# A four-layer graph network on one core: in the first attention layer, the product of a node's own features with its share moves from VectorE to GpSimd

## The reference

```python
s2 = jnp.concatenate([src, ar])          # edges, then one loop from each node to itself
d2 = jnp.concatenate([dst, ar])
...
a = jnp.exp(logit - m[d2])
denom = jax.ops.segment_sum(a, d2, num_segments=n)
alpha = a / denom[d2]                    # the shares, 4 heads
out = jax.ops.segment_sum(alpha[:, :, None] * xl[s2], d2, num_segments=n)
out = out.mean(axis=1) + b_gat
...                                      # normalize, gamma, beta, elu
x = _layernorm(x + that)
```

## Time and profile before

| what | value |
|---|---|
| time of 3 runs, median | 12803.6 us (12781.44 to 12825.93) |
| the profiled execution, its own time | 12791.1 us |
| its span in the trace | 12789.4 us |
| busy over the span: VectorE (DVE) | 6375.9 us, 50% |
| GpSimd (POOL) | 7493.3 us, 59% |
| TensorE (PE) | 6448.9 us, 50% |
| ScalarE (ACT) | 2885.5 us, 23% |
| mean granted TensorE clock | 0.717 of full speed |

### The profile page before, as it was taken

How to read it: one execution, slowest core, us unless ns; L and a number is a source line. 1 busy time by engine, 2 the same in 40 slices (tenths; PEclk the granted TensorE clock), 3 DMA queues, 4 the chain that set the end, 5 groups by cost and what they waited for, 6 DMA issues and landing times. The chain is left out here.

```text
span 12789.4 us, 75437 instructions
## 1 busy us (share of the span) xinstructions
PE 6448.9 (50%) x17662; PEld 2860.9 (22%) x17662; DVE 6375.9 (50%) x12622; ACT 2885.5 (23%) x5100; POOL 7493.3 (59%) x7050
## 2 busy tenths in 40 slices
PE   3432454455555886545454531345665575650276
PEld 1110222222222443222122210122222232330133
DVE  2110254444443333545454568436999994440486
ACT  1210322222222332222221210111000453220143
POOL 4667265666675443657566767666775003557487
PEclk8665777676767998767676765566666897765688
DMA  3520122111112443222222222222111342222243
GB/s 89 152 72 10 43 71 58 53 52 56 55 55 70 164 164 114 74 68 78 69 80 63 82 73 78 57 65 47 35 34 27 122 151 71 59 54 48 70 130 95
DMA packets 899857, 961.94 MB, mean 75 GB/s; under 512 B 480972, under 2 KB 535422, under 8 KB 886866
## 3 DMA queue, kind: packets, MB, share of 16 engines
q1 hardware_dynamic: 674034, 814.55, 19.4%
q0 software_dynamic: 225376, 142.56, 6.2%
HBM read 491.45 MB, written 542.49 MB: 81 GB/s over the span
## 5 line engine op out<-in xcount | busy, mean ns | idle before, releaser
L649 POOL DMA_INDIRECT gathered<-hop,place_of_source x1564 | 1610.4, 1030 | 1141.5 <-DVE weighted L694 474.0
L649 POOL DMA_INDIRECT gathered<-u,place_of_source x1564 | 1665.1, 1065 | 821.9 <-issue 480.0
L708 DVE SCALAR_TENSOR_TENSOR sums<-sums,same_as_before,weighted 128x64 f32<-128x64 f32 x3510 | 997.8, 284 | 193.0 <-DVE sums L708 29.4
L649 POOL DMA_INDIRECT gathered<-x,row_of_source x782 | 799.9, 1023 | 492.9 <-issue 238.6
L670 PE MATMUL bank<-of_first,ident 128*128 128x512 f32 (+1 forms) x1176 | 796.2, 769 | 561.8 <-issue 324.3
L1493 PE MATMUL bank<-glr,pair_turned 128*128 128x512 f32 x782 | 655.1, 935 | 447.9 <-issue 241.9
L435 PE MATMUL bank<-dense_tmp,mean 128*128 128x512 f32 x980 | 634.1, 775 | 448.6 <-issue 304.6
L435 PE MATMUL bank<-dense_a,center 128*128 128x512 f32 x588 | 441.1, 885 | 737.2 <-DVE dense_a L453 356.4
L1885 POOL DMA_INDIRECT out_dram<-attend_out,node_to_write x392 | 561.6, 1433 | 234.4 <-ACT attend_out L1806 114.9
L397 DVE COPY dense_out<-bank 128x512 f32<-128x512 f32 x392 | 261.0, 687 | 835.2 <-remote 712.9
L649 POOL DMA_INDIRECT gathered<-x_with_place,src_index x391 | 405.6, 1037 | 407.4 <-DVE weighted L694 280.9
(11 more groups left out here) (412 smaller groups left out, 14920.0 us busy)
## 6 DMA issues: line engine op xcount, KB each, us to landing
head_sums<-head_sums SPq DMA_DIRECT2D x98, 1024.0 KB
y<-conv_out SPq DMA_DIRECT2D x294, 256.0 KB
conv_out<-y SPq DMA_DIRECT2D x245, 256.0 KB
hop<-sums SPq DMA_DIRECT2D x196, 256.0 KB
cat<-hop SPq DMA_DIRECT2D x196, 256.0 KB
u<-conv_out SPq DMA_DIRECT2D x196, 256.0 KB
x<-dense_out SPq DMA_DIRECT2D x194, 256.0 KB
x<-dense_out SPq DMA_DIRECT2D x97, 272.0 KB
```

The lines of the kernel that those rows point to most:

```text
L649: return e.indirect_dma_start(out=into, out_offset=None, in_=tab, in_offset=bass.IndirectOffsetOnAxis(ap=index, axis=0), bounds_check=top, ...
L708: e.scalar_tensor_tensor(s[:, k, :], b, go[:, t:t + 1], m[:, k, :], ALU.mult, ALU.add).then_inc(st.summed.handle, 1)
```

## The change

The own product is taken out of VectorE's program into a function, `own_product`. In the first attention layer (`v2`) GpSimd calls it for all 49 groups; in the second layer VectorE still does, at the same place. GpSimd's gather `first_heads` stands behind the 49 products. Waits, operands and the semaphore `owned` are the same as before.

```diff
@@ -1820,6 +1820,15 @@
+            def own_product(e, g):
+
+                l, c = g % LANES, slice(g * K8, (g + 1) * K8)
+                if g >= 5:
+                    e.wait_ge(*turned_in(g - 5))
+                e.wait_ge(*(mine_in[l](16 * (g // LANES + 1)) if v2 else lanes[l].loaded[0](16 * (g // LANES + 1))))
+                e.tensor_tensor(heads_of(O[g % 5][:]), each_head(mine[l], K8), per_head(lg[:, HEADS:, c], K8),
+                                ALU.mult).then_inc(owned.handle, 1)
+
@@ -1874,10 +1883,11 @@
                     for g in range(NG):
+                        if v2:
+                            own_product(e, g)
+                            continue
                         if g == NG - 4:
                             first_heads()
-                        if v2:
-                            continue
@@ -1886,7 +1896,9 @@
-                    if not v2:
+                    if v2:
+                        first_heads()
+                    else:
@@ -1917,11 +1929,8 @@
                         steps.to(due(g, 0.6))
-                        if g >= 5:
-                            e.wait_ge(*turned_in(g - 5))
-                        e.wait_ge(*(mine_in[l](16 * (g // LANES + 1)) if v2 else lanes[l].loaded[0](16 * (g // LANES + 1))))
-                        e.tensor_tensor(heads_of(o[:]), each_head(mine[l], K8), per_head(lg[:, HEADS:, c0:c0 + K8], K8),
-                                        ALU.mult).then_inc(owned.handle, 1)
+                        if not v2:
+                            own_product(e, g)
                         steps.to(due(g, 0.8))
```

## The result

The changed kernel takes 13004.34 us (median of 4 runs, 12973.66 to 13025.25) against 12814.76 us for the kernel before, run beside it (4 runs, 12781.44 to 12828.5). The ratio is 1.015, 95% interval 1.012 to 1.0179, or 154 to 229 us slower. The direction was forecast; the size, 81 us on 12803.6, was not, and 13004 lies above the range's 12975.

The account below looks back on a forecast made before the run. VectorE, 97.0% busy, bounds the stage at 14.05 us per group; 11.35 + 4.4 + 0.1 = 15.85 us, 1.80 more over 49 groups, gives +88 us: 12885 us, range 12770 to 12975.

Parts of the forecast that it names:

- exclude each other: GpSimd's product and VectorE's two-input SBUF instructions never overlap, so their times add: 15.85 us per group, +88 us.
- L489 bore it: GpSimd gets in behind the product of features and shares, ahead of L489, which shows longer or idle time before it.
- VectorE's own work: VectorE's work per group in the first attention layer falls from 13.63 to 11.35 us without the own product.
- Rival 1: GpSimd and VectorE run side by side in the first attention layer: -100 us, 12695 us; chance 0.18.
- rival 2: GpSimd's reads go into gaps of VectorE's in the first attention layer: -4 us, 12795 us; chance 0.08.
- The hold: GpSimd's own product of 128x2048 in each group: 4.4 us, the middle between its two bounds.
- the lower end: GpSimd's product takes 2.94 us if its second input costs nothing.
- the upper: GpSimd's product takes 5.8 us if its second input costs as much as the first.
- k: Remainder per group beside VectorE's work and GpSimd's product: between -0.69 and 0.42 us, taken as 0.1.
- come late at VectorE: In the side-by-side case, chains of small steps late in half of the 14.05 us group: -60 instead of -112 us.

Follow-up runs that it names:

- run 4: The change, with GpSimd's product of a group also waiting until VectorE has added group g-2: 15.21 us a group.
- run 1: The change, with the own product left out on both engines and GpSimd filling the heads buffers with zeros once: 13.66 us a group.
- run 8: The change, with eight more 128x512 matmuls per group on TensorE into an unused bank: 17.54 us a group.
- runs 5 to 7: L484 moved behind the next group's product of features and shares, in the kernel before, the change, and the kernel without own product: 14.25, 16.00, 12.07 us a group.
- run 3: GpSimd takes four of the own product's eight columns (128x1024), VectorE the other four at the old place: 16.59 us a group.

## Why the prediction was wrong

**What held.** VectorE was the bound. GpSimd's product and VectorE's two-input steps exclude each other, now shown in both directions. The product came in behind the product of features and shares in three groups of four, and L489 bore it. VectorE's own work fell nearly as said: 11.65 us a group, forecast 11.35 (of the 0.3, 0.16 are the mean over the whole stage, 13.63 in place of 13.79, and 0.14 the product's 2.14 in place of 2.28). Rival 1 (side by side) and rival 2 (in pieces) did not occur.

**The hold was sized too high, 4.4 us.** In the change VectorE's busy time per group is 14.99 - 11.65 = 3.34 us more than without a product, and GpSimd's instruction alone takes 3.68 (run 4). That is 0.7 us above the lower end, 2.94, and 2.1 below the upper, 5.8. The Trainium skill's 4497 ns (GPSIMD Engine Reference, section 3.1), for an add of as many elements, is 0.8 us more than this product with both inputs broadcast took; the measurement decides. By this term alone the forecast would have been 49 x 1.1 = 52 us too high.

**The step that failed is k**, "at most the 0.42 us in which VectorE is idle anyway", taken as 0.1. It was 2.68 us. I bounded the idle time after the change by the idle time before it. But the product that was taken out was also what VectorE did while TensorE and ScalarE worked between L453 and L484. The trace of before had it, first VectorE and then ScalarE, whose L444 gives L484 its input:

```profile
10313.77 0.69 DVE L453 SCALAR_TENSOR_TENSOR attend_a<-attend_a,attend_xT 128x512 f32<-128x512 f32 x1
10314.38 2.04 DVE L1916 SCALAR_TENSOR_TENSOR head_sums<-head_sums,same_as_before 128x256 f32<-128x256 f32 x4
10316.34 2.29 DVE L1923 TENSOR_TENSOR heads<-own_rows,logits 128x2048 f32<-128x2048 f32 x1
10319.08 2.29 DVE L1934 TENSOR_TENSOR heads<-heads,head_sums 128x2048 f32<-128x2048 f32 x1 [0.46 <-DVE heads L1923]
10321.29 0.68 DVE L484 TENSOR_TENSOR attend_aT<-bank,attend_tmp 128x512 f32<-128x512 f32 x1
```
```profile
10319.40 1.16 ACT L444 ACTIVATE attend_tmp<-attend_tmp 128x512 f32<-128x512 f32 x2
```

L484 comes 6.8 us after the end of L453 (10314.46), but the two L444 that the two L484 need had both ended by 10320.56, so the chain was covered with only 0.7 us to spare. On the mean of the 40 groups the first L444 ends 0.64 us (0.03 to 1.24) before the first L484 starts. So of 2.28 us taken out ahead of it, 2.28 - 0.64 = 1.64 turn into waiting; run 1 has 1.68 in front of L484. Rival 1 says that the chains "come late at VectorE" in half of it; that belonged into every case, the likeliest one too. The sum that the runs show, per group:

| term | forecast | measured | from |
|---|---|---|---|
| product off VectorE | -2.28 | -2.14 | 13.79 to 11.65, run 1 |
| GpSimd's hold | +4.4 | +3.34 | 11.65 to 14.99 |
| idle time, product gone | -0.32 | +1.57 | 0.43 to 2.00, run 1 |
| idle time, GpSimd's product added | 0 | +0.68 | 2.00 to 2.68 |
| sum | +1.80 | +3.45 | 14.22 to 17.67 |

What the forecast's own mechanism, the hold for the product, was worth is 3.34 - 2.14 = 1.20 us a group, or 59 us; the uncovered chain, 1.57 + 0.68, is 110 us more. So the direction was right for the reason given. Had the hold been sized right, the forecast would have been 52 us lower and further off: that error hid half of what the other left out. Over 49 groups the measured sum is 169 us, and less at the stage's start, where no chain steps run yet: 160 in the trace. It also says what rival 1 would have been worth: 0.56 us a group, 27 us, and not 100. Had GpSimd cost nothing at all, the change would have been within the 0.3% of no change.

**What stays open.** The last 0.68 us lie in the chain: on the mean of the 40 groups the way from the end of L453 to L484 is 5.96 us in run 1 and 6.65 in the change. With the clock at full (run 8) it is still 6.48, so why it is longer isn't shown. And the difference of medians (190 us) is 30 more than the stage's 160; the rest of the program scatters by more than that between executions, and nothing here shows that the change reaches it.

## What to carry to other kernels

An instruction that is moved off a full engine leaves a gap that is worth its time only if nothing ends later than the gap: look for what the engine's next instruction waits for, through the other engines, and move the waiting step along with it (runs 5 to 7: one line decided whether 2.28 us were worth 0.56 or 2.18). GpSimd is no free second VectorE for work on SBUF: a product of 128x2048 that VectorE does in 2.28 us shut it out for 3.3 us when GpSimd did it. On a full VectorE that loses, for all of it (17.67 us a group, or 16.00 with L484 late) and for half (16.59), against 14.22; placing it into idle time made it cheaper (15.21), not cheap enough. And read the stage, not the kernel: two executions of the same stages differed by 53 us ahead of a stage that changed by 160.

## What the runs showed of the hardware

GpSimd's 128x2048 fp32 product with both inputs broadcast takes 3.68 us undisturbed and up to 5.68 when it finds VectorE in a two-input step. VectorE's steps that wait for it count as busy in the trace, with their durations lengthened (0.54 to 3.90 us). GpSimd's fill of 128x2048 takes 1.81 us and leaves VectorE's two-input steps alone, but holds up a tensor-scalar step. The granted clock fell from 0.96 to 0.85 in the stage when VectorE's holds left TensorE idle for a stretch of some 5 us in each group, and was at 1.00 with eight matmuls in the gap (run 8). In run 3 it was 0.82, with idle stretches of at most 4.0 us. The row of the change:

```profile
10417.84 0.90 PE L379 MATMUL bank<-ident,heads 128*128 128x128 f32 x4 [5.05 <-ACT attend_xT L389]
```
